# ScalarE makes the source one-hots and the first normalised rows; the first table is stored in five parts

## The chip, the cores and the metric

The kernel runs on one core of a Trainium2 chip. Its time is the device time of one execution, in microseconds (us); the figure to predict is the median over the runs. One execution was taken by the hardware profiler, and all rows below are from it.

The engines are TensorE (PE in the rows; PEld is its weight load), VectorE (DVE), ScalarE (ACT), GpSimd (POOL) and SyncE (SP, which here only issues DMAs). Each runs its own instructions in order, and they wait for one another by semaphores.

## The reference

The input is a table x of 3125 nodes by 256 values and a list of 53125 edges (source, destination, weight), sorted by destination. The computation is two layers, each with a graph network, an attention over all nodes and a feed-forward network with experts:

```
xn = layernorm(x)
x = x + gcn_two_hops(xn, edges, weight) + linear_attention(xn)
x = x + experts(layernorm(x))
xn = layernorm(x)
x = x + gin_two_layers(xn, edges) + linear_attention(xn)
x = x + experts(layernorm(x))
```

Only the first of these lines matters here. Each node has a degree, the sum of the weights of the edges into it (plus 1). One hop of the graph network takes the rows of a table at the source of each edge, multiplies them by the edge's weight, and sums them at its destination; rows are scaled by one over the square root of the degree before and after. Two hops follow each other.

## The kernel before, in words

Nodes are cut into T = 25 tiles of 128, edges into 416 chunks of 128; 8 chunks are one round, so there are 52 rounds (ROUNDS). A chunk's sum is a TensorE product of gathered rows with a one-hot of destinations.

**Degree sums** (`degrees`, `degree_sums`, `degree_products`). VectorE clears buffers (L1460 to L1471), among them VB, which holds the sums: four partitions to 0 (L1462), then one to 1 (L1465). Then each of 52 rounds is one VectorE instruction that makes 8 one-hots (L619), 8 TensorE products (L602), and an addition into VB (L632). Beside the last 25 rounds `statistics_beside` takes the mean and variance of one tile of x each (L1481).

**First rows** (`first_statistics`, `first_rows`). VectorE gathers the statistics (L1486), TensorE transposes the degree sums (L819), and roots are asked of ScalarE (`root`, L1216) and inverted on VectorE (`one_over_root`, L1435). VectorE then normalises 25 tiles of x into N (L1503). ScalarE multiplies the first A_ROWS = 15 of them by the inverse root of the degree (L1235) and VectorE the last 10 (L1508), into R. SyncE stores R to the first table in DRAM with two DMAs, one of 15 tiles and one of 10. Meanwhile TensorE transposes the inverse roots of the degrees (L826) and the normalised rows (L813), and ScalarE copies both out (L1239, L1226). When all are copied VectorE multiplies them (L1552) and starts hop 1.

**Hops** (`gather_pass`, `product_pass`, `add_pass`). GpSimd waits until the table is written and then issues one gather DMA for each chunk (L494): 416 in hop 1 and 416 in hop 2, into a ring of two rounds. The gather for chunk k of round r waits until the product of chunk k of round r-2 is done. VectorE makes the weighted one-hot of each chunk (L674) and adds each round's sum (L692). TensorE does the products (L555).

**Built beside the hops.** A dense bf16 adjacency is built meanwhile for a later layer: 208 subs of two chunks, half of them beside hop 1 and half beside hop 2, in 36 rounds of each hop, up to three subs in a round; hop 1 has them in rounds 2 to 10, 14 to 22, 26 to 34 and 38 to 46. For each chunk VectorE makes a cell one-hot (L1654, 500 wide) and a source one-hot (L1655, 128 wide) in rings of four, TensorE multiplies the two (L875), and VectorE adds each sub to a slab (L1666), which is cleared first (L1677).

Beside hop 1 TensorE also makes keys and values, half a tile a round (L840); ScalarE copies each and squares it (L1250, L1251) and gives the root for it (L1216); VectorE reduces and scales (`normalise_kv`, L1516 to L1523). In rounds 0 and 1 VectorE computes the numbers of cells (`spread_subs`, `cell_numbers`) and `choose_path` behind them.

The instruction order of each engine is written out by hand:

```
class Steps: add() counts an instruction, settle() waits for all counted, do() is both
sp.wait_ge(table_sbuf[0], A_ROWS)          # store tiles 0..14 of the table
sp.wait_ge(rows_scaled, T - A_ROWS)        # store tiles 15..24
pe.wait_ge(pool_step, 7)                   # so does VectorE ahead of its first instruction
```

## Time and profile before

| | us |
|---|---|
| median of three runs | 2993.53 (2991.62 to 2995.46) |
| the profiled execution | 2993.78 |
| its span in the trace | 2992.0 |
| PE busy | 2478.4 (83%) |
| DVE busy | 1299.7 (43%) |
| POOL busy | 866.6 (29%) |
| ACT busy | 454.3 (15%) |

The span is what the trace covers; the device time has 1.8 us more around it. Starts in the rows count from the start of the span. Busy shares are means over stages that have different limits: POOL works almost only in the two hops, which lie between 133 and 1233 us, and PE is busy nearly throughout from 1309 us on.

### The profile page before, as it was taken

To read this page: it belongs to the slowest core of one execution; us is meant where nothing else is said; L and a number is where in the kernel's file an instruction comes from. 1 tells how busy PE (TensorE), PEld (TensorE's weight loads), DVE (VectorE), ACT (ScalarE), POOL (GpSimd) and SP (SyncE) were. 2 spreads that over 40 slices of the span, in tenths; PEclk is the share of its full clock that TensorE was granted. 3 is DMA by queue.
4 is the path that set the end of the run, shared out by engine and by line. 5 is a ranking of instruction groups with operands and counts; after the bars stand their busy time and mean duration, and the time that the engine had idled before them with its cause. 6 is when DMAs were issued, how large, how long until landed. Compare 5 with 4: busy or idle time off the path is not lost.

```text
span 2992.0 us, 33704 instructions
## 1 busy us (share of the span) xinstructions
PE 2478.4 (83%) x12264; PEld 1717.7 (57%) x12264; DVE 1299.7 (43%) x3544; ACT 454.3 (15%) x963; POOL 866.6 (29%) x912
## 2 busy tenths in 40 slices
PE   4577777775666666689969998999999999999999
PEld 3456655654555555567745565565555556566665
DVE  8877867756765756442572124122000003131221
ACT  0201111101000000032231103330000010413222
POOL 0177777774777777320010000110000000000000
PEclk9989999987987988779989999999999999989999
DMA  3134344343434344110022221022111100000001
GB/s 105 58 101 135 103 139 139 104 139 110 125 119 140 103 139 139 46 50 0 27 74 70 65 74 38 32 85 70 57 50 50 36 1 4 18 11 11 11 11 43
DMA packets 77650, 211.87 MB, mean 71 GB/s; under 512 B 16445, under 2 KB 33845, under 8 KB 76073
## 3 DMA queue, kind: packets, MB, share of 16 engines
q0 software_dynamic: 40800, 111.47, 12.6%
q1 hardware_dynamic: 36681, 98.17, 9.9%
q8 instruction: 103, 1.69, 0.2%
q14 instruction: 66, 0.54, 0.1%
HBM read 169.10 MB, written 40.47 MB: 70 GB/s over the span
## 4 chain that ended last, share of the span: by engine, by line
PE 63%; DVE 15%; DMA 8%; issue 6%; POOL 5%; ACT 2%; DVEq 1%; SPq 0%; ACTq 0%; POOLq 0%
PE ps L1109 16%; PE ps L1145 13%; DMA rows<-table,src_i 8%; PE ps L1081 7%; PE ps L555 6%; POOL rows L494 5%; PE ps L1203 5%; PE ps L976 3%; PE ps L987 3%; DVE onehot L674 2%; DVE NN L1666 2%; DVE NN L1654 1%; PE ps L875 1%; PE ps L1165 1%; PE ps L813 1%
## 5 line engine op out<-in xcount | busy, mean ns | idle before, releaser
L494 POOL DMA_INDIRECT rows<-table,src_i x832 | 812.5, 977 | 390.1 <-issue 303.6
L555 PE MATMUL ps<-onehot,rows 128*128 128x128 f32 x3328 | 551.4, 308 | 213.0 <-DMA rows<-table,src_i 187.8
L555 PEld LDWEIGHTS ps<-onehot,rows 128*128 128x128 f32 x3328 | 521.1, 219 | 324.2 <-issue 213.5
L1109 PE MATMUL ps<-AS,WA 128*128 128x400 f32 (+1 forms) x768 | 257.8, 498 | 12.5 <-ACT NN L1347 6.1
L875 PE MATMUL ps<-NN 128*128 128x500 bf16 x416 | 169.1, 406 | 116.2 <-DVE NN L1655 100.6
L674 DVE TENSOR_SCALAR onehot<-iota_w,rel,wgt 128x128 f32<-128x128 f32 x848 | 230.1, 361 | 2.8 <-DVE iota_w L714 1.6
L1109 PEld LDWEIGHTS ps<-AS,WA 128*128 128x128 f32 x768 | 148.0, 193 | 121.2 <-ACT NN L1347 6.7
L1109 PE MATMUL ps<-NN,WA 128*128 128x400 f32 (+1 forms) x640 | 213.5, 495 | 1.0 <-ACT rows L1360 0.7
L2079 DVE SCALAR_TENSOR_TENSOR X<-ps,WA,X 128x256 f32<-128x256 f32 x150 | 72.6, 484 | 272.1 <-PE ps L1203 272.1
L1347 ACT ACTIVATE AS<-ps,small 128x400 f32<-128x400 f32 (+1 forms) x224 | 131.2, 586 | 334.7 <-PE ps L1109 334.7
L1109 PEld LDWEIGHTS ps<-NN,WA 128*128 128x128 f32 x640 | 122.4, 192 | 88.9 <-issue 1.6
L2023 DVE SCALAR_TENSOR_TENSOR AS<-ps,small,AS 128x408 f32 x32 | 20.3, 643 | 345.9 <-PE ps L1145 345.1
L692 DVE TENSOR_TENSOR AS<-AS,ps 128x256 f32 x104 | 43.9, 422 | 278.5 <-PE ps L555 278.4
L1666 DVE TENSOR_TENSOR NN<-NN,ps 128x500 f32 x208 | 140.3, 675 | 54.5 <-issue 22.5
L1654 DVE TENSOR_SCALAR NN<-WB,AS 128x500 bf16<-128x500 f16 x416 | 151.1, 363 | 0.3
L1145 PE MATMUL ps<-WA,NN 128*128 128x408 bf16 x768 | 137.1, 336 | 0.0
L1145 PE MATMUL ps<-onehot,NN 128*128 128x408 bf16 x768 | 136.1, 336 | 0.0
L1203 PE MATMUL ps<-WA,AS 128*128 128x256 f32 x600 | 135.6, 389 | 0.0
L875 PEld LDWEIGHTS ps<-NN 128*128 128x128 bf16 x416 | 43.4, 104 | 139.8 <-DVE NN L1666 98.2
L1203 PEld LDWEIGHTS ps<-WA,AS 128*128 128x128 f32 x600 | 104.2, 192 | 31.4 <-issue 13.1
L1655 DVE TENSOR_SCALAR NN<-WB,AS 128x128 bf16<-128x128 f16 x416 | 116.5, 280 | 0.0
L793 POOL CAST rows<-WA 128x512 bf16<-128x512 f32 x5 | 4.7, 931 | 376.2 <-DVE WA L2002 376.2
(353 smaller groups left out, 3071.5 us busy)
## 6 DMA issues: line engine op xcount, KB each, us to landing
adjacency<-NN SPq DMA_DIRECT2D x8, 2550.0 KB, 9.3
onehot<-adjacency SPq DMA_DIRECT2D x40, 510.0 KB, 3.5
WA<-adjacency SPq DMA_DIRECT2D x40, 510.0 KB, 3.5
rows<-table,src_i POOLq DMA_INDIRECT x832, 2.7
table<-NN SPq DMA_DIRECT2D x10, 640.0 KB, 3.3
table<-WA SPq DMA_DIRECT2D x25, 256.0 KB, 2.0
WA<-in_experts SPq DMA_DIRECT2D x6, 768.0 KB, 4.1
X<-in_x SPq DMA_DIRECT2D x1, 3072.0 KB
```

Source lines behind the costliest of these rows:

```text
L494: nc.gpsimd.indirect_dma_start(slot_of(h, j, k), None, table[h - 1][:, :], bass.IndirectOffsetOnAxis(index, 0)).then_inc(gathered[h - 1][( ...
L555: mm = nc.tensor.matmul(EDGE[j % 2][:, c * P:(c + 1) * P], row[:, c * P:(c + 1) * P], onehot[:, j % 2 * U + k, :], start=(k == 0 and c == ...
L674: nc.vector.tensor_scalar(onehot[:, buffer * U + k, :], iota_w[:, :], rel[:, bass.ds(c, 1)], wgt[:, bass.ds(c, 1)], ALU.is_equal, ALU.mult ...
L875: nc.tensor.matmul(build_bank(s)[:, 0:CELLS], sources_in[:, n % CELL_RING, :], cells[:, n % CELL_RING, :], start=(j == 0), stop=(j == 1)). ...
L1081: mm = nc.tensor.matmul(EDGE[c][:, 0:SLABW], rows16, pieces[i % 4][:, n, :], start=(t == 0 and part == 0), stop=(t == T - 1 and part == 2))
L1109: mm = nc.tensor.matmul(o[:, 0:n.stop - n.start], weights[:, k, c * P:(c + 1) * P], src[:, k, n], start=(k == 0), stop=(k == chunks - 1))
L1145: mm = nc.tensor.matmul(banks[c][:, 0:SLABW], hidden16(t)[:, part, f], pieces[i % 4][:, n, :], start=(t == 0 and part == 0), stop=(t == T ...
L1203: mm = nc.tensor.matmul(o[:, 0:D], h2[:, k, t * P:(t + 1) * P], w[:, 2, k, :], start=(k == 0), stop=(k == KC - 1))
L1347: nc.scalar.activation(dst[:, c, n], o[:, 0:n.stop - n.start], ACT.Relu, bias=bias[:, c:c + 1]).then_inc(pa_free, 1)
L1654: nc.vector.tensor_scalar(cells[:, n % CELL_RING, :], iota500, cell_of[:, n:n + 1], None, ALU.is_equal).then_inc(cells_ready, 1)
L1655: nc.vector.tensor_scalar(sources_in[:, n % CELL_RING, :], iota500[:, 0:P], source_in[:, n:n + 1], None, ALU.is_equal).then_inc(cells_read ...
L1666: nc.vector.tensor_tensor(part, part, build_bank(s)[:, 0:CELLS].rearrange("p (t n) -> p t n", n=SUBW), ALU.add).then_inc(slab_added, 1)
```

## The change

- The two fills of VB go from VectorE to GpSimd, behind its first fill and ahead of those that TensorE and VectorE wait for at their start.
- The statistics of x are taken beside rounds 6 to 30 of the degree sums, gathered beside rounds 31 to 39 (three tiles a round), and the root is asked in round 40. In round 42 VectorE inverts it and makes the shift, minus mean times inverse root. From then on ScalarE normalises the 25 tiles, x times scale plus shift.
- The table is stored in five DMAs of five tiles, in the order of groups 3, 0, 4, 1, 2; groups 3 and 4 are VectorE's.
- ScalarE makes the source one-hots in both hops, each with two instructions: the absolute difference of the source and a counter, then relu(1 - that). The second waits for the first. TensorE waits for cells and sources separately.

```diff
@@ sync
-            sp.wait_ge(table_sbuf[0], A_ROWS)
-            load(sp, rows_of_table(0, 0, A_ROWS), R[:, 0:A_ROWS, :], table_written[0])
-            sp.wait_ge(rows_scaled, T - A_ROWS)
-            load(sp, rows_of_table(0, A_ROWS, T), R[:, A_ROWS:T, :], table_written[0])
+            for done, count, g in ((rows_scaled, 1, 3), (table_sbuf[0], 1, 0), (rows_scaled, 2, 4), (table_sbuf[0], 2, 1), (table_sbuf[0], 3, 2)):
+                sp.wait_ge(done, count * GROUP)
+                load(sp, rows_of_table(0, g * GROUP, (g + 1) * GROUP), R[:, g * GROUP:(g + 1) * GROUP, :], table_written[0])
@@ gpsimd
             nc.gpsimd.memset(X[:, T - 1, :], 0.0).then_inc(x_zeroed, 1)
+            nc.gpsimd.memset(VB[0:PARTS, :], 0.0).then_inc(sums_cleared, 1)
+            pool.wait_ge(sums_cleared, 1)
+            nc.gpsimd.memset(VB[0:1, :], 1.0).then_inc(sums_cleared, 1)
@@ tensor, build_tile
-                pe.wait_ge(cells_ready, 2 * n + 2)
+                pe.wait_ge(cells_ready, n + 1)
+                pe.wait_ge(sources_ready, n + 1)
@@ scalar
+            root(rstd)
+            act.wait_ge(scales_ready, 1)
+            for t in range(T):
+                nc.scalar.activation(N[:, t, :], X[:, t, :], ACT.Identity, scale=rstd[:, t:t + 1],
+                                     bias=sc[:, 200 + t:201 + t]).then_inc(xn_ready, 1)
             root(dnode[:, 0:T])
-            root(rstd)
...
+            def sources_of(subs):
+
+                for s in subs:
+                    if s == 0:
+                        act.wait_ge(sub_diag, 2)
+                    for n in (2 * s, 2 * s + 1):
+                        if n >= CELL_RING:
+                            act.wait_ge(built, n - CELL_RING + 1)
+                        hot = sources_in[:, n % CELL_RING, :]
+                        nc.scalar.activation(hot, iota500[:, 0:P], ACT.Abs, scale=-1.0, bias=source_in[:, n:n + 1]).then_inc(source_step, 1)
+                        act.wait_ge(source_step, n + 1)
+                        nc.scalar.activation(hot, hot, ACT.Relu, scale=-1.0, bias=ones[:, 0:1]).then_inc(sources_ready, 1)
+
+            for r in range(ROUNDS):
+                t, half = divmod(r, 2)
                 b = t % 2
-                if t >= 2:
-                    act.wait_ge(kv_used, t - 1)
-                for half in range(2):
+                sources_of(subs_of(1, r)[2:])
+                if t < T:
+                    if t >= 2 and half == 0:
+                        act.wait_ge(kv_used, t - 1)
                     o = A.next()
                     part = slice(half * 512, (half + 1) * 512)
                     nc.scalar.copy(kv[:, b, part], o[:, :]).then_inc(kv_ready, 1)
                     nc.scalar.activation(kvsq[:, b, part], o[:, :], ACT.Square).then_inc(pa_free, 1)
-                root(sc[:, 256 + 32 * b:256 + 32 * b + 16])
+                sources_of(subs_of(1, r + 1)[0:2])
+                if t < T and half == 1:
+                    root(sc[:, 256 + 32 * b:256 + 32 * b + 16])
...
+            for r in range(ROUNDS):
+                sources_of(subs_of(2, r))
@@ vector, degrees
-                st.add(nc.vector.memset(VB[0:PARTS, :], 0.0))
                 st.add(nc.vector.tensor_copy(iota16, iota_w[:, :]))
                 st.settle()
-                st.add(nc.vector.memset(VB[0:1, :], 1.0))
+                dve.wait_ge(sums_cleared, 2)
@@ vector, statistics_beside
-                t = r - (ROUNDS - T)
-                if t == 0:
+                first, aggregates, ready = 6, 31, 42
+                if r == first:
                     dve.wait_ge(x_loaded, 32)
-                if t >= 0:
+                if first <= r < first + T:
+                    t = r - first
                     st.add(nc.vector.bn_stats(stats[:, t, :], X[:, t, :]))
-
-            def first_statistics():
-                st.settle()
-                for t in range(T):
-                    st.add(nc.vector.bn_aggr(mv[:, t, :], stats[:, t, :]))
-                st.settle()
+                if r == aggregates:
+                    st.settle()
+                for t in range(3 * (r - aggregates), min(3 * (r - aggregates) + 3, T)):
+                    if t >= 0:
+                        st.add(nc.vector.bn_aggr(mv[:, t, :], stats[:, t, :]))
+                if r == ready - 2:
+                    st.settle()
+                    nc.vector.tensor_scalar(rstd, mv[:, :, 1], LN_EPS, None, ALU.add).then_inc(asked, 1)
+                if r == ready:
+                    one_over_root(rstd)
+                    nc.vector.scalar_tensor_tensor(out=shift, in0=mv[:, :, 0], scalar=-1.0, in1=rstd,
+                                                   op0=ALU.mult, op1=ALU.mult).then_inc(scales_ready, 1)
@@ vector, first_rows
-                nc.vector.tensor_scalar(rstd, mv[:, :, 1], LN_EPS, None, ALU.add).then_inc(asked, 1)
-                one_over_root(rstd)
-                for t in range(T):
-                    nc.vector.tensor_scalar(N[:, t, :], X[:, t, :], mv[:, t, 0:1], rstd[:, t:t + 1],
-                                            ALU.subtract, ALU.mult).then_inc(xn_ready, 1)
@@ vector, cells_of
-                    nc.vector.tensor_scalar(sources_in[:, n % CELL_RING, :], iota500[:, 0:P], source_in[:, n:n + 1], None,
-                                            ALU.is_equal).then_inc(cells_ready, 1)
```

## Rows read from the trace of the kernel before

**Rows 1.** The page: chain that ended last, shares of the span, by engine.
```profile
PE 63%; DVE 15%; DMA 8%; issue 6%; POOL 5%; ACT 2%; DVEq 1%; SPq 0%; ACTq 0%; POOLq 0%
```

**Rows 2.** Waits of POOL (us, times, longest); its gathers (min/median/max ns, first, last).
```profile
POOL rows L494 <- PE ps L555: 86.5, 284, 0.3
...
L494 POOL DMA_INDIRECT rows<-table,src_i x832: 942/946/3908, 133.5 to 1226.6; - x167
```

**Rows 3.** Timeline of the start: start us, us, engine, line, operation [idle before, releaser].
```profile
0.80 0.31 POOL L744 MEMSET X<- 128x256 f32 x1 [0.29 <-POOLq L2133]
1.05 0.20 POOL L745 MEMSET ident<- 128x128 f32 x1
...
2.15 0.13 POOL L755 IOTA small<- 128x1 f32 x1
...
6.90 0.07 DVE L1402 MEMSET rel<- 128x8 f32 x1 [6.76 <-DMA AS<-in_dst_rounds]
...
15.35 2.83 DVE L1462 MEMSET VB<- 4x3328 f32 x1 [0.63 <-issue]
...
19.00 2.83 DVE L1465 MEMSET VB<- 1x3328 f32 x1 [0.75 <-DVE AS L1463]
...
21.77 0.55 DVE L1468 CAST AS<-wgt 128x416 bf16<-128x416 f32 x1
```

**Rows 4.** Timeline of the degree sums: two rounds without statistics, and the end.
```profile
38.83 0.28 DVE L632 TENSOR_TENSOR VB<-VB,ps 4x128 f32 x1
...
41.61 0.28 DVE L632 TENSOR_TENSOR VB<-VB,ps 4x128 f32 x1
...
108.14 0.27 DVE L632 TENSOR_TENSOR VB<-VB,ps 4x128 f32 x1
...
109.43 2.82 PE L819 MATMUL ps<-ident,VB 4*128 4x4 f32 x25 [1.72 <-DVEq L1473]
109.46 1.76 DVE L1486 BATCH_NORM_AGGREGATE small<-small 128x2 f32<-128x6 f32 x25 [0.38 <-DVE base_i L645]
```

**Rows 5.** Timeline from the roots to the first gathers.
```profile
113.76 0.19 DVE L1500 TENSOR_TENSOR small<-small 128x25 f32<-128x25 f32 x1
...
114.72 6.09 ACT L1235 ACTIVATE AS<-NN,small 128x256 f32<-128x256 f32 x15 [1.23 <-DVE NN L1503]
...
120.83 4.76 SPq L220 DMA_DIRECT2D table<-AS  x2
...
122.47 2.72 DVE L1508 TENSOR_SCALAR AS<-NN,small 128x256 f32<-128x256 f32 x10
...
133.53 1.14 POOL L494 DMA_INDIRECT rows<-table,src_i  x1 [108.59 <-issue]
...
137.08 6.89 DVE L1552 TENSOR_TENSOR AS<-NN,VB 128x3200 f32<-128x3200 f32 x2 [6.34 <-ACTq L1228]
...
137.48 3.91 POOL L494 DMA_INDIRECT rows<-table,src_i  x1 [0.30 <-issue]
```

**Rows 6.** Windows while the table is stored: the last figure is GB/s.
```profile
122.00:124.00 2.00, 2.00 (x12) 1.96 (x10) 1.89 (x8) 1.41 (x3) 0.00 (x0) 1.00 1.05 348
```

**Rows 7.** Timeline of hop 1, rounds 1 to 4: root, first slab, product, gather.
```profile
167.79 0.60 ACT L1251 ACTIVATE AS<-ps 128x512 f32<-128x512 f32 x1
...
170.18 0.22 ACT L1216 ACTIVATE small<-small 128x16 f32<-128x16 f32 x1 [1.78 <-DVE small L1517]
...
183.78 0.61 PE L555 MATMUL ps<-onehot,rows 128*128 128x128 f32 x4
...
186.81 0.95 POOL L494 DMA_INDIRECT rows<-table,src_i  x1 [0.30 <-issue]
```

**Rows 8.** Waits of PE, 185 to 270 us (hop 1, rounds 3 to 10).
```profile
PE ps L875 <- DVE NN L1655: 12.6, 8, 3.6
```

**Rows 9.** Timeline of POOL: first and last of 80 stretched gathers beside L1654 or L1655.
```profile
182.97 1.04 POOL L494 DMA_INDIRECT rows<-table,src_i  x1 [0.30 <-issue]
...
1173.72 1.09 POOL L494 DMA_INDIRECT rows<-table,src_i  x1 [0.30 <-issue]
```

14 lines of the change are left out of this document (7 added, 7 removed).

## The prediction, written before the change was run

> **What bounds the kernel now.** I read the chain that ended last first. It gives TensorE 63% of the span and GpSimd 5% [rows 1], and by that GpSimd looks unimportant. Then I read who waits for whom, over the two hops. The reader should see there that GpSimd never waits for anything: of its 832 gathers 284 follow a product of TensorE, and the longest of those waits is 0.3 us, which is the ordinary space between two gathers; a gather takes 0.942 to 0.946 us, so one starts each 1.25 us, from 133.5 to 1226.6 us [rows 2]. So in both hops the pace is the issue of gathers. TensorE, VectorE and ScalarE run behind it, up to two rounds behind, and what they do cheaper is worth nothing by itself. A change is worth something there only if it lets the first gather start earlier, or makes gathers shorter. Behind the hops the work is the same in both kernels and bound by TensorE, so it only moves. Ahead of the first gather stands a serial stretch of 133.5 us, where VectorE is the bound.
>
> So the sum has five terms: the start, the degree sums, the table, what is given back in hop 1, and the length of gathers. It is made against the profiled execution, 2993.78 us with a span of 2992.0; that lies 0.25 us above the median, 2993.53, so I take the difference off the median.
>
> **1. The fills of VB.** VectorE fills at 15.35 and at 19.00 us, 2.83 us each, with a small cast and a settle between them, and starts the next work at 21.77 [rows 3]. Without them the cast can start at 15.35 at the latest, lasts 0.15, and with the same settle of 0.75 the work starts at 16.25: 5.5 us earlier. What is added: GpSimd fills 256 columns in 0.31 and 128 in 0.20 us [rows 3], that is 0.86 ns a column, so 2.95 us for 3328, twice, with a wait of some 0.1 between: 6 us. They stand ahead of the seven steps that VectorE and TensorE wait for, which ended at 2.3 us [rows 3] and now end at 8.3. VectorE's first instruction started at 6.90, when a DMA had landed, and now starts at 8.3: 1.4 us late. The load of x is issued from the fill ahead of them and does not move. Net: 4.1 us gained.
>
> **2. The degree sums.** Two rounds without statistics take 41.61 - 38.83 = 2.78 us [rows 4]. The 25 statistics only change their rounds, which costs nothing. The 25 aggregations took 1.76 us, and were hidden behind TensorE's transposes, 2.82 us from 109.43 [rows 4]: taking them away there gives nothing. Beside the rounds three of them are 0.21 us, where VectorE has about 0.07 us free in a round (its one-hots and its addition fill the rest); so 0.14 times 8.3 rounds, 1.2 us. Round 31's settle, round 40's settle and small operation, and round 42's reciprocal, settle and shift are small instructions of 0.2 to 0.3 us and their waits: 0.7 us. Together 1.9 us lost; the ends are 0.7 (aggregations free) and 2.6 (all paid in full). With term 1 the end of the sums (108.14 before [rows 4]) comes 2.2 us earlier.
>
> **3. Rows and table.** From round 42 on there are nine more rounds, 12.5 us, and then 5.5 us to the degree's inverse root, which is ready at 113.95 [rows 5]. ScalarE needs 25 rows at 0.406 us (15 in 6.09 [rows 5]), 10.2 us, and is otherwise idle: hidden, with some 8 us to spare. What VectorE's own normalisation held up goes. ScalarE's 15 rows start at about 114.0 instead of 114.72 and end at 120.1 instead of 120.8; ScalarE's copies, the transposes between them, VectorE's product at 137.08 and the first products of hop 1 all follow ScalarE, so they gain 0.7 us and not more. The ten rows of VectorE took 2.72 us from 122.47 [rows 5]; now they start at 114.0, and five of them are there at 115.4.
>
> The two stores were issued at 120.83 and, from the last of the ten rows, about 125.2 [rows 5]; while they ran the DMA engines moved 348 GB/s [rows 6]. 3.28 MB at that rate is 9.4 us: from 121.8 to 131.3, landing at about 131.8 and the first gather at 133.53 [rows 5]. Five stores start at 115.4, bytes flow a microsecond later, and each group is ready before the ones ahead of it have moved (groups 0, 4, 1, 2 at 116.2, 116.8, 118.2 and 120.2, against 118.4, 120.3, 122.1 and 124.0). So the path is the bound, the bytes end at 125.9, and the first gather starts at 128.0. This is 5.5 us earlier. Ends: 4.5, if five issues leave gaps, and 6.5. With terms 1 and 2 GpSimd starts 7.7 us earlier, the rest of hop 1 only 2.9 us (2.2 + 0.7).
>
> **4. What hop 1 gives back.** These 4.8 us of extra lead must fit into the ring. VectorE's setup (cell numbers, then a fill of the slab) makes TensorE late in round 2. Gather 39, chunk 6 of round 4, needs the product of chunk 6 of round 2. That product ended at 184.39 (183.78 + 0.61) and the gather started at 186.81 [rows 7]: a slack of 2.4 us, the smallest of the hop. So 4.8 - 2.4 = 2.4 us are lost here. There is a new wait as well: in round 1 ScalarE finishes its square at 168.39 and gave the root at 170.18, right when asked [rows 7]. Now it makes four source one-hots in between, each two dependent instructions of 0.22 us (the root) to 0.41 us (a row of 256), so 0.7 us a one-hot and 2.8 in all, to 171.2. The root is 1 us late, and VectorE stands still for it, with choose_path and the slab's fill behind. GpSimd loses this too: 3.4 us in all; the ends are 1.5 and 5.5. In rounds 3 to 10 TensorE waits for VectorE's source one-hots (12.6 us in 8 waits [rows 8]), so taking six of them a round from VectorE makes that slack larger, and later rounds have slacks of 8 us and more. No second stall. So at its first gathers GpSimd is 7.7 us early, and from round 4 on 4.3.
>
> ScalarE's load in the other rounds: six one-hots at 0.7 us, 4.2, and a copy and a square, 1.2, in a round of 10. Hidden; if that cover went, each microsecond above 10 a round would count in 36 rounds a hop. The VectorE time that is freed, 416 short instructions, lies beside gathers throughout: zero.
>
> **5. Shorter gathers.** The median gather takes 0.946 us [rows 2]. The largest lengthening is beside L1552 (3.91 us instead of 0.94 [rows 5]) and stays, as that instruction stays. But 80 gathers between 182.97 and 1173.72 us took over 0.98 us beside L1654 or L1655 [rows 9], with 8.7 us more than 0.945 each between them. The two have as many instructions, but L1655 is 128 columns wide and L1654 500; half would be 4.4 us and a fifth 1.8. I take 2.5, nearer to the widths, with ends 0 and 6.
>
> The row of the 3.91 us gather shows GpSimd held up for as long as a VectorE instruction lasts. The Trainium skill, page "SBUF — State Buffer", section "SBUF: two separate sides", gives a rule for it: VectorE in a two-port mode, or with two SBUF inputs, and GpSimd take one shared port pair exclusively, and descriptors of GpSimd's DMAs wait for it. ScalarE has its own ports by that page, so one-hots moved to it would cost GpSimd nothing. By that rule term 5 is a gain; without the rule it is zero, and the total would be 4.3 us.
>
> **Sum.** 4.1 - 1.9 + 5.5 - 3.4 + 2.5 = 6.8 us; 2993.53 - 6.8 = 2986.7 us.
>
> **Rivals.**
> - *Gathers get no shorter, or round 4 takes back all of the table's gain.* For it: the stretched gathers are only 10% of all, and the slack of 2.4 us is a fact. Against it: they cluster beside the two lines. Then the time is 2993.53 - 4.3 = 2989.2; with the stall at 5.5, 2991.3. Within 0.2%. Chance 0.33.
> - *The lengthening is mostly due to L1655, and ScalarE's late root does not hold.* For it: VectorE has two short instructions instead of one beside each gather, and each can catch it. Then terms 4 and 5 are 2.4 and 6, and the time 2993.53 - 11.3 = 2982.2. Chance 0.15.
> - *GpSimd's fills are slower than the slope of its short ones.* They stand ahead of everything, so each microsecond of them counts from the point where they pass the DMA's landing. Terms 2 to 5 give 2.7 and term 1 5.5 at most. Slower than before from 6.90 - 1.1 - 1.2 + 8.2 = 12.8 us for the two, 6.4 each, that is 1.9 ns a column. At 3.5 ns a column they take 23.3 us, and the time is 2993.53 + 10.5 = 3004. For it: no row has a GpSimd fill over 256 columns. Against: the rows lie on a line, and it is VectorE's own rate. Chance 0.06.
> - *ScalarE's pair becomes the pace.* Its one-hots are in the loop of a ring of four with TensorE. It decides from (10 - 1.2) / 6 = 1.47 us a one-hot; at 2.0 a round of hop 1 takes 13.2, and 36 such rounds lose some 112 us, less at most two rounds of the ring, 20 us, in each of the four blocks: 32, so 3019. Against: nothing on ScalarE of 128 columns takes over 0.41. Chance 0.03.
>
> **How the numbers follow.** The forecast has 0.43. The measurement tells about 0.2%, 6 us, from no change. Faster by more than that: nearly all of the second rival, three quarters of the forecast's case (6.8 is just above it) and a few of the first, 0.52. Slower: the last two, 0.07. The rest within, 0.41. The range: the first rival's end and the second's, 2981.5 to 2992.
>
> **What would show it.** The first VectorE instruction at 8.3 us and L1468 at about 17.7; the first gather at about 125.8, and at 186.81 - 4.3 = 182.5 the 39th, with a wait of GpSimd for TensorE of 2 to 4 us ahead of one gather in round 4, the only one in the hops; hop 2's first gather 5 to 6 us earlier than before; far fewer than 80 gathers over 0.98 us beside the cells' one-hots. ScalarE's one-hots at under 0.4 us an instruction, no table load in the hops. I would be wrong if GpSimd waited in many rounds, if the first gather were not 6 us early, or if the stretch from the last gather to the end were not as long as before.

## The result and the profile after

The changed kernel takes 2981.92 us in the median of six runs (2980.35 to 2982.86), the kernel before 2993.18 beside it: a ratio of 0.9959, with a 95% interval of 0.9947 to 0.9971. The medians differ by 11.3 us, and the interval allows 8.7 to 15.9, where 6.8 were forecast. 2981.92 lies 0.4 above the lower end of the range, but the ratio applied to the 2993.53 that the forecast started from gives 2981.3, just below that end, and a second run of the changed kernel had 2980.58. The profiled execution of the changed kernel took 2982.86 us, 10.9 below the one before, and its span is 2980.4, 11.6 below; the other 0.7 lie outside the trace. Line numbers have moved: L1468 is now L1494, L1500 is L1534, L1235 is L1243, L1552 is L1581, and the cells' one-hot L1654 is L1683.

The start, the end of the degree sums and the first gathers, from the timeline of the kernel after. These rows answer to [rows 3 to 5].

```profile
1.05 2.87 POOL L745 MEMSET VB<- 4x3328 f32 x1
...
3.97 2.86 POOL L747 MEMSET VB<- 1x3328 f32 x1
...
8.17 0.07 DVE L1429 MEMSET rel<- 128x8 f32 x1 [8.03 <-POOL small L758]
...
15.90 0.16 DVE L1489 CAST AS<-iota_w 128x128 f16<-128x128 f32 x1
...
16.10 0.63 DVE L1494 CAST AS<-wgt 128x416 bf16<-128x416 f32 x1
...
104.23 0.27 DVE L632 TENSOR_TENSOR VB<-VB,ps 4x128 f32 x1
...
105.20 2.83 PE L822 MATMUL ps<-ident,VB 4*128 4x4 f32 x25 [1.18 <-DVEq L1499]
...
109.46 0.18 DVE L1534 TENSOR_TENSOR small<-small 128x25 f32<-128x25 f32 x1
...
109.68 6.09 ACT L1243 ACTIVATE AS<-NN,small 128x256 f32<-128x256 f32 x15 [0.60 <-DVE small L1534]
...
111.11 5.26 SPq L221 DMA_DIRECT2D table<-AS  x5
...
123.86 1.14 POOL L494 DMA_INDIRECT rows<-table,src_i  x1 [98.24 <-issue]
...
132.51 6.89 DVE L1581 TENSOR_TENSOR AS<-NN,VB 128x3200 f32<-128x3200 f32 x2 [14.57 <-ACTq L1232]
...
132.81 4.00 POOL L494 DMA_INDIRECT rows<-table,src_i  x1 [0.30 <-issue]
```

The reader is to compare each start with its row before. The work behind the fills starts at 16.10 instead of 21.77 us, the last addition of the sums at 104.23 instead of 108.14, the inverse root at 109.46 instead of 113.76, the first gather at 123.86 instead of 133.53. Of a lead of 9.7 us the table gives 5.4: from inverse root to first gather it was 19.77 us and is 14.40. The 4.00 us gather stays with its VectorE product, as expected; L1581 is two instructions of 3.49 us, and each holds one gather (4.00 and 3.10 us).

Round 1's late root, and the gathers that bound the hops, from the timeline of the kernel after:

```profile
163.14 0.60 ACT L1274 ACTIVATE AS<-ps 128x512 f32<-128x512 f32 x1
...
166.25 0.40 ACT L1262 ACTIVATE NN<-NN,ones 128x128 bf16<-128x128 bf16 x1
...
166.55 0.20 ACT L1220 ACTIVATE small<-small 128x16 f32<-128x16 f32 x1
...
166.78 0.25 DVE L1462 RECIPROCAL small<-small 128x16 f32<-128x16 f32 x1 [1.23 <-ACT small L1220]
...
176.44 0.94 POOL L494 DMA_INDIRECT rows<-table,src_i  x1 [3.38 <-PE ps L555]
...
663.52 0.95 POOL L494 DMA_INDIRECT rows<-table,src_i  x1 [0.30 <-PE ps L555]
...
693.25 0.94 POOL L494 DMA_INDIRECT rows<-table,src_i  x1 [28.78 <-issue]
...
1213.42 0.94 POOL L494 DMA_INDIRECT rows<-table,src_i  x1 [0.30 <-issue]
```

The same three gathers of the kernel before (last of hop 1, first and last of hop 2):

```profile
671.79 0.95 POOL L494 DMA_INDIRECT rows<-table,src_i  x1 [0.30 <-PE ps L555]
...
701.37 0.94 POOL L494 DMA_INDIRECT rows<-table,src_i  x1 [28.63 <-issue]
...
1226.57 0.95 POOL L494 DMA_INDIRECT rows<-table,src_i  x1 [0.30 <-issue]
```

From the first to the last gather hop 1 takes 539.66 us (538.26 before) and hop 2 takes 520.17 (525.20 before). Hop 2 has no new start and no wait to lose; it is simply 5.03 us shorter. Where that is, the windows over hop 2 show, whose POOL figure is the busy time of the 416 gathers. First before, from 700 us:

```profile
700.00:1228.00 528.00, 343.75 (x1985) 292.11 (x1986) 321.82 (x1030) 2.28 (x6) 399.72 (x416) 0.84 0.40 124
```

then after, from 692 us:

```profile
692.00:1215.00 523.00, 353.85 (x1988) 297.54 (x1988) 287.60 (x822) 158.72 (x422) 394.72 (x416) 0.82 0.41 125
```

399.72 less 394.72 is 5.00 us: the whole gain of hop 2 lies inside the gathers. At 0.945 us each, 416 gathers would be 393.1, so 6.6 us of lengthening have become 1.6. Gathers over 0.98 us went from 59 to 15 in hop 2 and from 68 to 41 in hop 1. VectorE has 208 instructions fewer in the window, the source one-hots; ScalarE has them now, two for one.

ScalarE's pair, from the page of the kernel after; it is 393 and 401 ns where VectorE's one instruction took 280, and nothing waits for it long enough to matter:

```profile
L494 POOL DMA_INDIRECT rows<-table,src_i x832 | 805.6, 968 | 383.1 <-issue 293.3
...
L1260 ACT ACTIVATE NN<-WB,AS 128x128 bf16<-128x128 f16 x416 | 163.6, 393 | 342.0 <-PE ps L879 340.8
...
L1262 ACT ACTIVATE NN<-NN,ones 128x128 bf16<-128x128 bf16 x416 | 166.9, 401 | 13.5
```

Waits of TensorE from 176 to 262 us, the place of [rows 8]: the source one-hot has gone from the list, and the slab's addition has taken its place with 14.8 us. It costs nothing either, as GpSimd doesn't wait there from 180.4 us on (ahead of that lie its waits of round 4).

```profile
PE ps L879 <- DVE NN L1693: 14.8, 9, 3.0
```

The differences of the two traces add up so: start 5.67 gained, degree sums 1.76 lost, 0.39 gained ahead of the inverse root, table 5.37 gained, round 4's wait 3.07 lost (3.38 less the ordinary 0.30), 1.67 gained in the rest of hop 1 (1.40 longer in all, with the wait in it; the gathers were busy 1.87 us less, and a second wait of 0.50 us took 0.20 of that) and 5.03 in hop 2, 0.15 lost between the hops. That is 13.15. Behind the last gather the kernel after took 1766.98 us, the one before 1765.43: 1.55 lost, in work that is the same in both. Together 11.6, the difference of the spans.

**What runs when a long gather starts.** A gather and the cells' one-hot that was in flight when it started, first before, then after:

```profile
880.47 0.34 DVE L1654 TENSOR_SCALAR NN<-WB,AS 128x500 bf16<-128x500 f16 x1
880.59 1.04 POOL L494 DMA_INDIRECT rows<-table,src_i  x1 [0.30 <-PE ps L555]
```

```profile
733.03 0.33 DVE L1683 TENSOR_SCALAR NN<-WB,AS 128x500 bf16<-128x500 f16 x1
733.30 0.95 POOL L494 DMA_INDIRECT rows<-table,src_i  x1 [0.30 <-PE ps L555]
```

The reader is to see when each compare ends. The first ends 0.22 us after the start of its gather, and the gather is 0.10 us longer than 0.945; the second ends 0.06 us after it, and the gather has its ordinary length. Read over all traces of this case it comes out as a rule: of the 595 long gathers (over 0.98 us) of hop 2 in the 17 traces, 519 are longer than 0.945 us by the time from 0.13 us after their start to the end of the VectorE instruction in flight at that start, within 0.02 us. Of the 500-wide cell one-hots, in the 16 traces that have them, 353 started 0.08 to 0.19 us before a gather, and 349 of these gathers took over 0.96 us; 351 started 0.20 to 0.30 us before one, and 1 of those gathers did; 291 started between 0.02 us before and 0.03 us after, and 4 did. So the hold depends on when a compare starts. Before the change, the instruction in flight at the 59 long gathers of hop 2 was the cells' one-hot L1654 33 times, the weighted one-hot L674 19 times, the slab's addition L1666 5 times, and the source one-hot L1655 twice. After it the same two kinds remain, 13 and 2 times. The source one-hot itself held hardly any gather; taking it away moved the starts of the others.

### The profile page after: what moved, and what is told of

It is laid out like the page before. It is cut to its first block, busy times and chain, and to the rows that moved or that the text cites. A ratio compares the mean times of both kernels' runs of the same rounds, so it can differ in the third digit from the quotient of the medians.

```text
span 2980.4 us, 34334 instructions
## 1 busy us (share of the span) xinstructions
PE 2488.1 (83%) x12264; PEld 1712.6 (57%) x12264; DVE 1216.6 (41%) x3102; ACT 771.8 (26%) x1820; POOL 865.2 (29%) x914
## 4 chain that ended last, share of the span: by engine, by line
PE 65%; DVE 11%; DMA 11%; issue 6%; POOL 4%; ACT 2%; DVEq 1%; POOLq 0%; ACTq 0%
PE ps L1113 16%; PE ps L1149 13%; DMA rows<-table,src_i 10%; PE ps L555 8%; PE ps L1085 7%; PE ps L1207 5%; POOL rows L494 4%; PE ps L980 3%; PE ps L991 3%; PE ps L879 1%; DVE onehot L674 1%; PE ps L1169 1%; PE ps L843 1%; PE ps L816 1%; PE ps L1009 1%
## 5 line engine op out<-in xcount | busy, mean ns | idle before, releaser
L555 PE MATMUL ps<-onehot,rows 128*128 128x128 f32 x3328 | 557.8, 310 | 246.3 <-DMA rows<-table,src_i 217.3
L1260 ACT ACTIVATE NN<-WB,AS 128x128 bf16<-128x128 f16 x416 | 163.6, 393 | 342.0 <-PE ps L879 340.8
L674 DVE TENSOR_SCALAR onehot<-iota_w,rel,wgt 128x128 f32<-128x128 f32 x848 | 229.6, 363 | 2.8 <-DVE iota_w L714 1.6
L1262 ACT ACTIVATE NN<-NN,ones 128x128 bf16<-128x128 bf16 x416 | 166.9, 401 | 13.5
L1374 ACT ACTIVATE NN<-ps,small 128x400 f32<-128x400 f32 (+1 forms) x64 | 37.2, 585 | 474.2 <-PE ps L1113 474.2
L1683 DVE TENSOR_SCALAR NN<-WB,AS 128x500 bf16<-128x500 f16 x416 | 127.5, 361 | 0.3
```

Of the source, the lines that this page charges most:

```text
L555: mm = nc.tensor.matmul(EDGE[j % 2][:, c * P:(c + 1) * P], row[:, c * P:(c + 1) * P], onehot[:, j % 2 * U + k, :], start=(k == 0 and c == ...
L674: nc.vector.tensor_scalar(onehot[:, buffer * U + k, :], iota_w[:, :], rel[:, bass.ds(c, 1)], wgt[:, bass.ds(c, 1)], ALU.is_equal, ALU.mult ...
L1260: nc.scalar.activation(hot, iota500[:, 0:P], ACT.Abs, scale=-1.0, bias=source_in[:, n:n + 1]).then_inc(source_step, 1)
L1262: nc.scalar.activation(hot, hot, ACT.Relu, scale=-1.0, bias=ones[:, 0:1]).then_inc(sources_ready, 1)
L1374: nc.scalar.activation(dst[:, c, n], o[:, 0:n.stop - n.start], ACT.Relu, bias=bias[:, c:c + 1]).then_inc(pa_free, 1)
```

## The experiments

Each was compared with the kernel before on its own chip. The first four cut the change into parts, the next group looks for what makes gathers shorter, and the last ones for what round 4 takes back and for a better version. The changed kernel itself was run for the result and once more on the chip of the extra compares of 128 and 500 columns in f16 and of the early root; elsewhere a comparison with it crosses chips. "Hop 2" below is the time from its first to its last gather, and "long gathers" are those over 0.98 us in it.

**The fills alone**, in the kernel before:

```diff
             nc.gpsimd.memset(X[:, T - 1, :], 0.0).then_inc(x_zeroed, 1)
+            nc.gpsimd.memset(VB[0:PARTS, :], 0.0).then_inc(sums_cleared, 1)
+            pool.wait_ge(sums_cleared, 1)
+            nc.gpsimd.memset(VB[0:1, :], 1.0).then_inc(sums_cleared, 1)
...
-                st.add(nc.vector.memset(VB[0:PARTS, :], 0.0))
-                st.add(nc.vector.memset(VB[0:1, :], 1.0))
+                dve.wait_ge(sums_cleared, 2)
```

> The kernel before with one edit: GpSimd makes the two fills of VB. Theory (a fill costs more than its own 2.83 us, because each stood behind 0.63 to 0.75 us of issue, and the settle is nearly free): L1468's work starts at 16.1 us instead of 21.77, and everything behind it moves by 5.7 us; the first gather at 127.9, hop 2's last gather 5.7 us earlier, time 2987.6. Rival (the settle of 0.75 stays, as forecast): 17.4 us, everything moves by 4.1, time 2989.1.

Measured: 2992.15 us, ratio 0.9986 [0.9977, 0.9995]. In the timeline the work behind the fills starts here:

```profile
16.11 0.63 DVE L1471 CAST AS<-wgt 128x416 bf16<-128x416 f32 x1
```

That is 5.66 us earlier, and the first gather comes at 127.76, 5.77 earlier. So the forecast's 4.1 for this edit was too small, and the edit alone is worth its 5.7 us up to the first gather. The median shows 3.65 of them (2995.8 less 2992.15; the interval goes from 1.5 to 6.9), so the time does not decide between 5.7 and 4.1; the trace does. Hop 1 took 541.34 us in this trace against 538.26, without any wait in it: its gathers were busy for 415.85 us, against 412.76.

**ScalarE's source one-hots alone**, in both hops, in the kernel before:

```diff
-                pe.wait_ge(cells_ready, 2 * n + 2)
+                pe.wait_ge(cells_ready, n + 1)
+                pe.wait_ge(sources_ready, n + 1)
...
-                    nc.vector.tensor_scalar(sources_in[:, n % CELL_RING, :], iota500[:, 0:P], source_in[:, n:n + 1], None,
-                                            ALU.is_equal).then_inc(cells_ready, 1)
```

with `sources_of` and its calls as in the change.

> The kernel before with one edit: ScalarE makes the source one-hots in both hops. Theory (VectorE's narrow one-hots themselves lengthened the gathers beside them): first gather unchanged at 133.5; hop 2 from first to last gather 520.2 us instead of 525.2, hop 1 some 2 us shorter than 538.3; no wait of GpSimd for TensorE over 0.4 us; time 5 to 7 us under the kernel before, 2986 to 2988. Rival 1 (forecast, 2.5 us in all): 2990.7. Rival 2 (the gathers got shorter because of when they ran, not what ran beside them): no change of hop 2's 525.2, time 2993.

Measured: 2991.68 us, ratio 0.9985 [0.9976, 0.9994]. The first gather stays at 133.33, hop 1 takes 536.64, hop 2 takes 521.17 with 21 long gathers instead of 59. Hop 2 came out as expected, the time less so: 5 to 7 us were expected, and the medians differ by 4.1 (2995.8 less 2991.68; the interval goes from 1.8 to 7.2).

**All but ScalarE's source one-hots**, which VectorE makes again in the changed kernel:

```diff
                     nc.vector.tensor_scalar(cells[:, n % CELL_RING, :], iota500, cell_of[:, n:n + 1], None, ALU.is_equal).then_inc(cells_ready, 1)
+                    nc.vector.tensor_scalar(sources_in[:, n % CELL_RING, :], iota500[:, 0:P], source_in[:, n:n + 1], None,
+                                            ALU.is_equal).then_inc(cells_ready, 1)
```

> The changed kernel with VectorE making the source one-hots again, all else as changed. Theory: first gather at 123.9 as in the changed kernel; hop 2 from first to last gather 525.2 us again; hop 1 with a wait for TensorE of 2 to 3 us in round 4 and further ones later, since rounds 3 to 10 of VectorE are no longer relieved; time 6 to 8 us above the changed kernel, 2988 to 2990. Rival (sources are worth 2.5 us only): 2984.5.

Measured: 2987.45 us, ratio 0.9972 [0.9961, 0.9983]. The first gather is at 124.48 and hop 2 is back at 524.68 us, with 53 long gathers. Hop 1 takes 543.44 us, with four waits of GpSimd for products (2.58, 0.61, 1.43 and 0.95 us), as expected. The two halves of the change multiply to 0.9972 x 0.9985 = 0.9957, and the whole gave 0.9959: they add up, some 8.4 us for the start, the sums and the table, and some 4.5 for the one-hots.

**ScalarE's source one-hots in hop 2 only**, in the kernel before:

```diff
+                    if n < SUBS:
                         nc.vector.tensor_scalar(sources_in[:, n % CELL_RING, :], iota500[:, 0:P], source_in[:, n:n + 1], None,
-                                                ALU.is_equal).then_inc(cells_ready, 1)
+                                                ALU.is_equal).then_inc(sources_ready, 1)
```

> The kernel before with ScalarE making the source one-hots beside hop 2 only. Theory: hop 1 as before, 538.3 us from first to last gather; hop 2 520.2 instead of 525.2; time 5 us under the kernel before, 2988. Rival (no gather gets shorter): 2993.

Measured: 2997.22 us, ratio 1.0006 [0.9997, 1.0015]. This is a miss. Hop 2 did shorten, to 521.22 us with 25 long gathers, but hop 1, where VectorE has the same instructions as before, took 541.06 with 415.56 us of gathers, as in the run of the fills alone, and the stretch behind the last gather 1769.49 against 1765.43. So hop 1 varies by some 3 us from trace to trace, and the trace of the kernel before may stand at its low end. The stretches behind the hops, alike in all these kernels, lie between 1763.8 and 1772.1 us. A single trace can hide 4 us so; that the median shows no gain at all stays open.

**An extra short compare on VectorE**, in the changed kernel, into memory that nobody reads:

```diff
+                    spare = A2[:, 4096 if n < SUBS else 0:][:, n % CELL_RING * 250:n % CELL_RING * 250 + 250].bitcast(BF16)
+                    nc.vector.tensor_scalar(spare[:, 0:P], iota500[:, 0:P], source_in[:, n:n + 1], None, ALU.is_equal)
                     nc.vector.tensor_scalar(cells[:, n % CELL_RING, :], iota500, cell_of[:, n:n + 1], None, ALU.is_equal).then_inc(cells_ready, 1)
```

> The changed kernel, and VectorE makes a second 128-wide one-hot for each chunk into a spare buffer that nobody reads, so that VectorE's work is as before while ScalarE does the source one-hots. Theory (a narrow VectorE one-hot holds up gathers): hop 2 from first to last gather 524 to 525 us, with 50 or more gathers over 0.98 us, instead of 520.2 with 15. Rival (the gathers got shorter because VectorE and TensorE wait for one another differently, not by VectorE's instruction itself): 520 to 521 and about 20.

Measured: 2985.09 us, ratio 0.997 [0.9959, 0.9981], against 2980.58 for the changed kernel run beside it. The window over hop 2 in its trace:

```profile
692.00:1222.00 530.00, 350.39 (x1988) 296.34 (x1989) 322.67 (x1030) 159.05 (x422) 399.24 (x416) 0.83 0.40 123
```

The gathers' busy time is 399.24 us, as in the kernel before (399.72), though ScalarE still makes the source one-hots. So it is the presence of a short VectorE instruction there that makes gathers long; neither TensorE's new waits nor the earlier start has to do with it. But it does not hold them itself. Of the 44 long gathers of hop 2, 37 have the 500-wide cell one-hot L1685 in flight at their start, which is the same instruction as in the changed kernel, 6 the weighted one-hot, one the slab's addition and none the short L1684. One of the 37:

```profile
743.72 0.34 DVE L1685 TENSOR_SCALAR NN<-WB,AS 128x500 bf16<-128x500 f16 x1
743.84 1.04 POOL L494 DMA_INDIRECT rows<-table,src_i  x1 [0.30 <-PE ps L555]
```

The wide one starts 0.12 us before the gather, as in the kernel before. The extra instruction has moved it there: cell one-hots that start 0.08 to 0.19 us before a gather of hop 2 are 25 before the change, 14 after it and 27 here, and those that start 0.20 to 0.30 us before one, which is harmless, are 4, 44 and 6.

**The same, 500 wide:**

```diff
+                    nc.vector.tensor_scalar(spare, iota500, source_in[:, n:n + 1], None, ALU.is_equal)
```

> As the kernel with the extra 128-wide one-hot, but the extra one is 500 wide. If the length of the VectorE instruction decides, a gather is held longer and more often than by the narrow one: hop 2 over 526 us. If the number of instructions decides: 524 to 525, as with the narrow one. Rival (back-to-back wide one-hots do not hold gathers, as the remaining ones in the changed kernel hardly do): 521.

Measured: 2988.47 us, ratio 0.9984 [0.9975, 0.9994]. The window over its hop 2, and the two wide compares by shape from 693 to 1213 us:

```profile
692.00:1222.00 530.00, 341.98 (x1988) 291.32 (x1988) 353.71 (x1033) 158.49 (x423) 396.07 (x416) 0.84 0.41 125
```

```profile
L1684 DVE TENSOR_SCALAR AS<-WB,AS 128x500 bf16<-128x500 f16 x208 | 78.8, 379 | 0.1
L1685 DVE TENSOR_SCALAR NN<-WB,AS 128x500 bf16<-128x500 f16 x208 | 76.8, 369 | 0.0
```

It adds more VectorE time than the short one (78.8 us for 208), and yet the gathers are held only 1.35 us more than in the changed kernel. Hop 2 takes 521.57 us with 22 long gathers, as the rival among the expectations had it. The time goes in hop 1 instead: seven waits of GpSimd for products, 9.6 us in all, and hop 1 takes 543.32 us, because VectorE's work no longer fits beside the gathers there. So what the gathers lose does not grow with VectorE's busy time. By the starts this is as it should be: of the twice as many wide compares in this hop 2, 18 start 0.08 to 0.19 us before a gather and 83 start 0.20 to 0.30 us before one.

**Other extra instructions in the same place**, in the changed kernel, each line for one run. First 128 columns of an f32 counter, and then 127:

```diff
+                    nc.vector.tensor_scalar(spare[:, 0:128], iota_w[:, 0:128], source_in[:, n:n + 1], None, ALU.is_equal)
```

> The changed kernel with one more VectorE one-hot a chunk into a spare buffer: 128 wide, from the f32 counter to bf16. Theory (two-port form holds gathers, as the narrow f16 one did): hop 2 524 us and over 40 gathers above 0.98 us. Rival (only the f16 form does): 520.5 to 521.5 and about 20.

```diff
+                    nc.vector.tensor_scalar(spare[:, 0:127], iota_w[:, 0:127], source_in[:, n:n + 1], None, ALU.is_equal)
```

> As the kernel with the extra 128-wide f32 to bf16 one-hot, but 127 wide. By the Trainium skill, page Vector Engine (DVE) Microarchitecture Reference, an odd count with unequal sizes has no two-port form, so the instruction lasts longer and leaves the pair alone: by it hop 2 is 520.5 to 521.5 us with about 20 gathers above 0.98 us though VectorE is busier. Rival (any further short instruction of VectorE holds gathers): hop 2 524 or more.

Measured: 2986.29 us, 0.9975 [0.9964, 0.9985], and 2985.16 us, 0.9971 [0.9959, 0.9983]. Hop 2 takes 525.06 and 524.62 us, with 41 and 48 long gathers. By shape from 693 to 1213 us the extra instruction is, in the even and in the odd run:

```profile
L1684 DVE TENSOR_SCALAR AS<-iota_w,AS 128x128 bf16<-128x128 f32 x208 | 60.9, 293 | 0.1
```

```profile
L1684 DVE TENSOR_SCALAR AS<-iota_w,AS 128x127 bf16<-128x127 f32 x208 | 60.7, 292 | 0.1
```

The odd width changed neither the duration nor the hold. As the two durations are the same, the run does not show that the odd one took another mode, and so it does not tell the two theories of these expectations apart. In both runs most long gathers have the 500-wide cell one-hot L1685 in flight (27 of 41 and 32 of 48), and few have the extra one (6 and 9).

Then 256 wide, the cell one-hot cut into two halves, and the short compare against a constant instead of a column:

```diff
+                    nc.vector.tensor_scalar(spare[:, 0:256], iota500[:, 0:256], source_in[:, n:n + 1], None, ALU.is_equal)
```

> The changed kernel with one more VectorE one-hot a chunk into a spare buffer, 256 wide in f16 (128 wide gave hop 2 524.7 us from first to last gather and 44 gathers over 0.98 us, 500 wide 521.6 and 22). If shortness is what holds gathers, 256 lies between: 522.5 to 524, 30 to 40. Rival (only the 128-wide form does): 521.6 and about 22.

```diff
-                    nc.vector.tensor_scalar(cells[:, n % CELL_RING, :], iota500, cell_of[:, n:n + 1], None, ALU.is_equal).then_inc(cells_ready, 1)
+                    nc.vector.tensor_scalar(cells[:, n % CELL_RING, 0:250], iota500[:, 0:250], cell_of[:, n:n + 1], None, ALU.is_equal)
+                    nc.vector.tensor_scalar(cells[:, n % CELL_RING, 250:500], iota500[:, 250:500], cell_of[:, n:n + 1], None, ALU.is_equal).then_inc(cells_ready, 1)
```

> The changed kernel with each 500-wide cell one-hot made by two instructions of 250, so twice as many instructions with the same columns and no extra buffer. If the count of short instructions decides: hop 2 523 us or more, over 30 held. Rival (it is the narrow one alone): 520.5 to 521.5 and about 20.

```diff
+                    nc.vector.tensor_scalar(spare[:, 0:P], iota500[:, 0:P], 5.0, None, ALU.is_equal)
```

> The changed kernel with one more 128-wide one-hot a chunk that compares with a constant in the instruction instead of a column read from SBUF. If the read of that column (from a second buffer) holds the gathers: hop 2 520.5 to 521.5. Rival (the instruction as such): 524.5 and over 40 held.

Measured in one run each: 2983.67, 2981.91 and 2988.24 us. What they say lies in hop 2 and not in these times:

| hop 2 in the trace | us | long gathers |
|---|---|---|
| before | 525.20 | 59 |
| after (two traces) | 520.17, 520.43 | 15, 18 |
| + 128 wide, f16, column | 524.71 | 44 |
| + 128 wide, f16, constant | 523.98 | 42 |
| + 128 wide, f32 | 525.06 | 41 |
| + 127 wide, f32 | 524.62 | 48 |
| + 256 wide, f16 | 525.09 | 55 |
| + 500 wide, f16 | 521.57 | 22 |
| cells in two halves | 522.46 | 41 |

The 256-wide one missed both of its expectations, the halves lie just below the 523 of theirs, and the constant agrees with its rival. An additional instruction of up to 256 columns costs 3.6 to 4.9 us of hop 2, whatever its input, the one of 500 columns 1.1 to 1.4, and two halves in place of one 2.0 to 2.3. With the 256-wide one and with the constant, too, it is mostly the cell one-hot that is in flight at the long gathers (31 of 55 and 29 of 42). So the differences come from how each sequence of instructions lies against the starts of the gathers; how that would be forecast for another sequence, these runs do not settle.

**The root ahead of the one-hots**, in round 1 of the changed kernel:

```diff
+                if r == 1:
+                    root(sc[:, 256 + 32 * b:256 + 32 * b + 16])
                 sources_of(subs_of(1, r + 1)[0:2])
-                if t < T and half == 1:
+                if 1 < r < 2 * T and half == 1:
                     root(sc[:, 256 + 32 * b:256 + 32 * b + 16])
```

> The changed kernel, and ScalarE gives the root of round 1 ahead of the four source one-hots of round 2 instead of behind them. Theory: the one wait of GpSimd for TensorE in round 4, 3.4 us in the changed kernel, shrinks by 1 to 1.2 us, the time by as much: 2981. Rival (VectorE's root was not late, the wait is the ring alone): 3.4 us again and no change.

Measured: 2981.49 us, ratio 0.9958 [0.9945, 0.9972]. The wait in round 4 shrank from 3.38 to 1.18 us:

```profile
174.46 1.03 POOL L494 DMA_INDIRECT rows<-table,src_i  x1 [1.18 <-PE ps L555]
```

Taken alone this would prove the late root. But **the changed kernel was run once more** on the same chip, with nothing altered:

> The changed kernel itself, for comparison on the same chip: 12 us under the kernel before, first gather at 123.9 us, hop 2 520.2 us from first to last gather.

Measured: 2980.58 us, ratio 0.9957 [0.9943, 0.997], and in its trace the root is late by less (0.64 us idle before the reciprocal, where the other execution had 1.23), and the wait in round 4 is short as well:

```profile
164.99 0.25 DVE L1462 RECIPROCAL small<-small 128x16 f32<-128x16 f32 x1 [0.64 <-ACT small L1220]
...
174.58 0.95 POOL L494 DMA_INDIRECT rows<-table,src_i  x1 [1.34 <-PE ps L555]
```

So the size of that wait varies between executions of one kernel, from 1.3 to 3.4 us, and putting the root first gains nothing that can be measured.

**Two stores instead of five**, in the changed kernel:

```diff
-            for done, count, g in ((rows_scaled, 1, 3), (table_sbuf[0], 1, 0), (rows_scaled, 2, 4), (table_sbuf[0], 2, 1), (table_sbuf[0], 3, 2)):
-                sp.wait_ge(done, count * GROUP)
-                load(sp, rows_of_table(0, g * GROUP, (g + 1) * GROUP), R[:, g * GROUP:(g + 1) * GROUP, :], table_written[0])
+            sp.wait_ge(table_sbuf[0], A_ROWS)
+            load(sp, rows_of_table(0, 0, A_ROWS), R[:, 0:A_ROWS, :], table_written[0])
+            sp.wait_ge(rows_scaled, T - A_ROWS)
+            load(sp, rows_of_table(0, A_ROWS, T), R[:, A_ROWS:T, :], table_written[0])
```

> The changed kernel with the table stored by two DMAs again, 15 tiles and then 10. The rows are ready as in the changed kernel, so only the form of the store differs. Theory: bytes start at 116.8 instead of 112 us and the first gather at 128.5 instead of 123.9, 4.6 later; the ring's wait in round 4 (1.3 to 3.4 us) is gone, so 1.5 to 3.3 us are left of it: 2984. Rival (the lead is worth its full size): 2985.5. Rival (the ring eats all of it): 2981.

Measured: 2984.21 us, ratio 0.9966 [0.9954, 0.9979]. The stores are issued from 115.80 us on instead of 111.11, and the first gather comes 4.76 us later than with five:

```profile
115.80 2.23 SPq L221 DMA_DIRECT2D table<-AS  x2
...
128.62 1.14 POOL L495 DMA_INDIRECT rows<-table,src_i  x1 [103.32 <-issue]
```

There is no wait in round 4 then, and the time is 2.3 and 3.6 us above the changed kernel's two medians, on other chips; the intervals of the ratios overlap. So nearly all of the table's gain, 4.76 of 5.37 us, comes from five stores in the order of readiness in place of two (number and order were not tried apart), and part of it is given back: hop 1 takes 534.57 us here, 2.5 to 5.1 less than behind five stores.

**A version meant to beat both**: GpSimd's fills moved behind the seven small steps that TensorE and VectorE wait for, and the five additions of the bias moved from beside rounds 2 to 10 of hop 1 to ahead of it, where VectorE stood idle.

```diff
-            nc.gpsimd.memset(VB[0:PARTS, :], 0.0).then_inc(sums_cleared, 1)
-            pool.wait_ge(sums_cleared, 1)
-            nc.gpsimd.memset(VB[0:1, :], 1.0).then_inc(sums_cleared, 1)
...
+            nc.gpsimd.memset(VB[0:PARTS, :], 0.0).then_inc(sums_cleared, 1)
+            pool.wait_ge(sums_cleared, 1)
+            nc.gpsimd.memset(VB[0:1, :], 1.0).then_inc(sums_cleared, 1)
             pool.wait_ge(cols_loaded, 16)
...
+            for g in range(GROUPS):
+                x = X[:, g * GROUP:(g + 1) * GROUP, :]
+                st.add(nc.vector.tensor_tensor(x, x, bias_b[:, :].unsqueeze(1).to_broadcast([P, GROUP, D]), ALU.add))
             dve.wait_ge(nt_ready, T)
...
-            for g in range(GROUPS):
-                beside_hop1[2 * g + 2] = lambda g=g: add_bias(g)
```

> The changed kernel with two more moves: GpSimd makes the fills of VB behind its seven first steps instead of ahead of them, and VectorE adds the bias to x (five instructions of 1.5 us with two inputs in SBUF) while it waits for the transposes ahead of hop 1 instead of beside rounds 2, 4, 6, 8 and 10. Theory: VectorE starts at 6.9 us instead of 8.2, so all moves by 1.3; the gathers that stood beside the bias, each up to 0.9 us longer, 3.7 us in all, are short, less what the bias now catches of the first gathers; the wait in round 4 is 1.3 to 3.4 as before. First gather at 122.6, hop 1 535 us, time 4 us under the changed kernel, 2977. Rival (GpSimd's lead meets the ring again, so hop 1 gives nothing): 2980.

Measured: 2976.82 us, ratio 0.9945 [0.9931, 0.9958]. It has the lowest median of all, 17 us below the kernel before on its chip; the interval of its ratio overlaps with the changed kernel's. From its timeline:

```profile
2.23 2.86 POOL L757 MEMSET VB<- 4x3328 f32 x1
...
5.15 2.86 POOL L759 MEMSET VB<- 1x3328 f32 x1
...
6.40 0.07 DVE L1429 MEMSET rel<- 128x8 f32 x1 [6.27 <-DMA AS<-in_dst_rounds]
...
6.43 1.81 DVE L1431 CAST rel<-rel 128x416 f32<-128x416 int32 x1
...
117.63 7.10 DVE L1579 TENSOR_TENSOR X<-X,bias_b 128x1280 f32<-128x1280 f32 x5
...
123.51 2.24 POOL L494 DMA_INDIRECT rows<-table,src_i  x1 [99.07 <-issue]
```

Both moves were made at once, so their shares are read from the trace. The gain lies where the bias was: hop 1 takes 533.32 us, against 537.10 to 539.66 in two traces of the changed kernel, and has no wait at all. Beside the five additions of the bias the changed kernel's gathers were 3.7 us longer in all than 0.945 each; here one gather is, by 1.3. The fills gave next to nothing: VectorE starts at 6.40 instead of 8.17 us, but its cast now takes 1.81 us and ends at 8.24, where the changed kernel has this:

```profile
8.20 0.38 DVE L1431 CAST rel<-rel 128x416 f32<-128x416 int32 x1
```

The cast ran beside GpSimd's second fill, which ended at 8.01. The first gather is only 0.35 us earlier.

## Why the forecast was right in direction and short in size

**The start.** Forecast 4.1, measured 5.67. GpSimd's fills took 2.87 and 2.86 us (forecast 2.95 each), and VectorE started at 8.17 (forecast 8.3). The failed step is "with the same settle of 0.75". Each of VectorE's two fills stood behind a space of its own, 0.63 and 0.75 us [rows 3]; I charged one of them again though both belonged to the fills. In the trace after, the cast ends at 16.06 and the next work starts at 16.10. The fills alone confirmed it, 5.66 us.

**The degree sums.** Forecast 1.9 lost, measured 1.76.

**Rows and table.** Forecast 5.5, measured 5.37 from inverse root to first gather; VectorE's product ahead of hop 1 (L1552, now L1581) followed with 4.57 us of the 9.67, as it hangs on ScalarE's copies. Two stores put back 4.76, so this step was right and for the stated reason.

**What hop 1 gives back.** Forecast 3.4 with one wait in round 4, measured 3.07 with one wait, at the 36th gather and not the 39th. The size agrees by luck: a second execution has 1.04 beyond the ordinary space, and of the term's two parts the late root (1.0) could not be measured when it was taken away. The slack of 2.4 us was read at the 39th gather, and a gather needs some 0.27 us from its product to its start in any case; at the 36th it was 2.98 us. That the ring takes back part of a lead stands, as with two stores there is no wait; the root's microsecond doesn't.

**Shorter gathers.** Forecast 2.5, measured 6.7 (5.03 in hop 2 and 1.67 in hop 1, the latter less sure, as hop 1 varies by more than that: against the two other traces with VectorE's source one-hots in hop 1 and no waits, 541.34 and 541.06 us, it would be about 4.6). This is the main failure, and the step is "I take 2.5, nearer to the widths". I split the lengthening between the two compares by their columns, as if each kept its share when the other goes. It doesn't: in hop 2 the long gathers had the 500-wide L1654 in flight 33 times of 59 and L1655 twice, and still the gain came with L1655's going, as that moved the starts of what was left. The extra 128-wide compare brings back 4.3 us of hop 2's 5.0 and the 500-wide one 1.1 (both against 520.43, the changed kernel on the same chip), and neither is a price of its own width. The 6 us were among the rivals ("mostly due to L1655"), and I gave them 0.15. The rule of the Trainium skill (page "SBUF — State Buffer", section "SBUF: two separate sides"), by which VectorE can shut GpSimd out of a port pair that they share, agrees with the traces: all 15 long gathers of hop 2 after the change have a VectorE instruction in flight at their start, and they last until 0.82 us after its end, within 0.02 us. By that section whichever of the two starts first has the pair for its whole instruction, and VectorE's form with two inputs in SBUF locks only against a GpSimd operation that reads SBUF, a condition that my forecast left out and that no run here tests. The rule says how long a gather is held that meets a compare; how many gathers meet one it doesn't say, and that is where my split went wrong.

**Behind the hops.** "Were not as long as before" was named as a way to be wrong, and it was 1.55 us longer in this trace. Since it differs by 8 us between traces of kernels that are the same there, it can't be put down to the change.

Of the rivals, *gathers no shorter* is refuted by the windows, *GpSimd's fills slower* and *ScalarE's pair as the pace* by their durations. The nearest was *mostly due to L1655*: its 2982.2 us lies 0.3 from the measured median, in part because a start that was 1.6 too small and the 1.55 us behind the hops cancel. Its reason, that each of VectorE's two short instructions can catch a gather, is only half right: with L1655 gone the gathers are short, but it was seldom the one that caught them.

## What to carry to other kernels

Where GpSimd's issue of gathers is the pace, look at which VectorE instruction is in flight when each gather starts, and how long it still runs. Moving one of VectorE's instructions to another engine can pay even at two instructions for one, but its price can't be told from its width or busy time, nor from whether it meets a gather itself; it shifts the others, so the sequence has to be run. Store a table in the order in which its parts are ready, but look at the ring behind it, which gives some of an early start back unless late work of another engine, here the bias, leaves the first rounds. Before reading a microsecond or two out of one trace, look at the same stretch in a second execution of the same kernel.

## What the runs showed of the hardware that was not expected

- A gather can be held by the VectorE instruction in flight at its start: 519 of the 595 long gathers of hop 2 end 0.82 us after that instruction, within 0.02 us. A one-hot of 0.34 us that starts 0.08 to 0.19 us ahead of a gather holds it (349 of 353); one that starts 0.20 to 0.30 us ahead doesn't (1 of 351), and ends at most 0.15 us after the gather's start.
- So an extra VectorE instruction costs by where it moves the others: 208 extra compares of 128 columns (287 ns each) cost 4.3 us in hop 2, and 208 of 500 columns (379 ns each) cost 1.1 us (both against the changed kernel's 520.43). Neither f16 against f32, nor a column against a constant, nor 127 against 128 columns changed the first figure by more than 0.8 us.
- A long VectorE instruction with two inputs from memory holds a gather through: 4.00 us instead of 0.95 beside the first of L1581's two instructions of 3.49 us, and 2.24 us at the first gather beside the bias additions. A VectorE fill of 4.3 us (L1704) held none of the 23 gathers that started under it in the changed kernel's trace; the longest took 0.95 us.
- It works the other way too: a VectorE cast of 128 x 416 from int32 took 1.81 us instead of 0.38 beside a GpSimd fill, and ended 0.23 us after it.
- A GpSimd fill costs by columns, 2.87 us for 3328 on four partitions and 2.86 on one, and VectorE's took 2.83 [rows 3].
